# Self-attention in eight blocks, four PSUM banks for the first pass, and inverted sums spread over partitions and multiplied in on POOL

## The reference, cut to what matters

```python
q, k, v = (_heads(q), _heads(k), _heads(v))          # (2, 16, 2048, 32)
attn = jnp.einsum('bhnd,bhmd->bhnm', q, k) * SCALE
attn = jax.nn.softmax(attn, axis=-1)
sa = _merge(jnp.einsum('bhnm,bhmd->bhnd', attn, v)) @ sa_proj_w.T
```

## Time and profile before

| what | us |
|---|---|
| three runs | 3642.99, 3648.21, 3652.91; median 3648.21 |
| the profiled execution | 3647.82 |
| its span, first to last instruction | 3646.0 |
| mean granted TensorE clock | 0.949 of full |

### The profile page before, as it was taken

How to read it: one execution, slowest core, us unless ns; L and a number is a source line. 1 busy time by engine, 2 the same in 40 slices (tenths; PEclk the granted TensorE clock), 3 DMA queues, 4 the chain that set the end, 5 groups by cost and what they waited for, 6 DMA issues and landing times. The chain is left out here.

```text
span 3646.0 us, 52480 instructions
## 1 busy us (share of the span) xinstructions
PE 3342.0 (92%) x16448; PEld 2093.6 (57%) x16448; DVE 2225.3 (61%) x3891; ACT 1551.9 (43%) x2794; POOL 1702.1 (47%) x507
## 2 busy tenths in 40 slices
PE   7998999999999999999999848898967599999999
PEld 5885544444444444444444336656536478888887
DVE  4445888888888878888888234767646532222222
ACT  3230566665666666666666613343432321111111
POOL 0001688887888888888888822343423100000000
PEclk9997999999999999999999968999958799999999
DMA  4447357365465646547444443343325741111110
GB/s 171 182 158 194 62 111 152 85 146 105 88 146 112 132 94 129 121 91 160 99 99 88 99 141 113 117 126 120 102 83 200 254 143 47 47 47 46 46 47 23
DMA packets 179012, 412.02 MB, mean 113 GB/s; under 512 B 20801, under 2 KB 43911, under 8 KB 159343
## 3 DMA queue, kind: packets, MB, share of 16 engines
q1 hardware_dynamic: 156271, 273.87, 24.7%
q0 software_dynamic: 18432, 134.23, 18.3%
q10 hardware_dynamic: 4096, 1.06, 0.1%
HBM read 146.08 MB, written 102.56 MB: 68 GB/s over the span
## 5 line engine op out<-in xcount | busy, mean ns | idle before, releaser
L1653 DVE TENSOR_REDUCE self_part_max<-self_first 128x1 f32<-128x512 f32 x2048 | 1278.1, 676 | 302.9 <-PE self_first L1510 299.6
L1611 ACT ACTIVATE self_expo<-self_second 128x512 f32<-128x512 f32 x2048 | 1068.2, 602 | 693.1 <-PE self_second L1526 654.4
L1459 POOL TENSOR_TENSOR self_pair_sum<-self_expo 128x2048 f32<-128x2048 f32 x192 | 882.9, 4598 | 119.2 <-ACT self_expo L1611 95.3
L1510 PE MATMUL self_first<-self_k,self_q 96*128 96x512 f32 x2048 | 886.0, 440 | 41.4 <-DVE self_part_max L1653 24.5
L1526 PE MATMUL self_second<-self_q,self_k 98*128 98x512 f32 x2048 | 814.7, 401 | 13.9 <-ACT self_expo L1611 13.9
L1510 PEld LDWEIGHTS self_first<-self_k,self_q 96*128 96x128 f32 x2048 | 395.5, 193 | 559.7 <-DVE self_part_max L1653 443.8
L1539 PE MATMUL self_weighted<-self_expo,self_v_sb 128*32 128x512 f32 x4096 | 546.3, 605 | 9.0 <-ACT self_unscaled L1623 6.8
L1526 PEld LDWEIGHTS self_second<-self_q,self_k 98*128 98x128 f32 x2048 | 389.5, 191 | 111.0 <-ACT self_expo L1611 48.7
L2005 DVE CAST mlp_h_high<-mlp_h 128x512 fp32r<-128x512 f32 x128 | 54.8, 428 | 507.9 <-PE mlp_out_sum L61 507.0
L1980 ACT ACTIVATE mlp_h<-mlp_hidden_sum,mlp_b_col 128x512 f32<-128x512 f32 x128 | 88.3, 690 | 603.0 <-PE mlp_hidden_sum L61 603.0
L1459 POOL TENSOR_TENSOR self_half_sum<-self_expo 128x2048 f32<-128x2048 f32 x64 | 293.0, 4583 | 88.2 <-ACT self_expo L1611 88.2
(11 more groups left out here) (165 smaller groups left out, 4180.5 us busy)
## 6 DMA issues: line engine op xcount, KB each, us to landing
self_half_sum<-self_pair_sum POOLq DMA_DIRECT2D x128, 1024.0 KB, 7.2
self_k<-k_t SPq DMA_DIRECT2D x96, 256.0 KB, 9.8
self_q<-q_t SPq DMA_DIRECT2D x93, 256.0 KB, 4.5
cross_q<-cross_r_high SPq DMA_DIRECT2D x256, 64.0 KB, 2.0
qkv_x<-in_x SPq DMA_DIRECT2D x8, 1024.0 KB, 5.4
v<-qkv_v_sb SPq DMA_DIRECT2D x32, 256.0 KB, 2.0
q_t<-qkv_r_high SPq DMA_DIRECT2D x32, 256.0 KB, 2.0
q_t<-qkv_r_low SPq DMA_DIRECT2D x32, 256.0 KB, 2.3
```

Of the source, the lines that this page charges most:

```text
L1459: nc.gpsimd.tensor_tensor(to, expo[:, t % p_slots], expo[:, (t + 1) % p_slots], ALU.add).then_inc(pair_done, 1)
L1510: nc.tensor.matmul(first[:, in_ring[n]], q[0:base, c % q_slots, a, s * P:(s + 1) * P], k[0:base, c // stages_per_group % 2, a, k0:k0 + TOK ...
L1611: nc.scalar.activation(expo[:, t % p_slots, a], second[:, n % ring], ACT.Exp, scale=scale).then_inc(exp_done, 1)
L1653: nc.vector.tensor_reduce(part_max[:, a * SUB + s, k:k + 1], first[:, in_ring[n]], AX_X, ALU.max).then_inc(first_read, 1)
```

## The change

- A stage has eight blocks instead of 16. In each, PE issues eight first-pass and eight second-pass tiles in turn and then weighs two key tiles, those of the block before. DVE and ACT follow the same order.
- The first pass gets a PSUM ring of four banks. The bank `total` is gone: `total` and the turned maxima are now uses of the second pass's ring of three (`s_uses`), so what comes three uses later in that ring waits for their readers. The turn comes after one first-pass tile, at the start of block 6.
- All three sums are added in one go at the end of block 1 of the next stage.
- ACT copies the weighted values into `mean` and, new, `total` into `inverse`. SP gathers one row of it for each head into `sums`, 16 columns on each of 128 partitions (four DMAs). DVE takes one reciprocal of that 128x16 tile in block 3. SP stores it to a DRAM scratch, waits for that, and loads it back into `inverse`, broadcast over the 32 partitions of each head (four DMAs).
- POOL multiplies `mean` by `inverse` (128x512), between its pairs 3 and 4 of the next stage.
- `pair_sum` and `half_sum` become four parts of one buffer, two of which change roles from stage to stage. POOL's wait for its own previous addition (`pair_done`, `n_adds * i`) now stands ahead of pair 0, and its wait for a sum ahead of pair 0 is gone.

The core of the diff:

```diff
-    blocks = n_k
-    per_block = heads
+    blocks = 8
+    per_block = n_seconds // blocks
...
-    turn_after = 2
-    ring = 3
+    turn_after = 1
+    f_ring = 4
+    s_ring = 3
     p_slots = 8
-    pieces = 8
+    share = heads * TOK // P
...
-    sums_at = {15: [(0, 0)], 2: [(-1, 1)], 3: [(-1, 2)]}
-    last_sum, invert_from, max_sent = 3, 5, 13
+    sum_block, take_sum_after = 1, 2 * per_block - 1
+    invert_at, max_sent_after = (3, 1), 55
...
+    def sum_parts(c):
+        return (0, 1, 2, 3) if c % 2 == 0 else (2, 1, 0, 3)
...
+    s_uses = []
+    for j in range(blocks):
+        for at in range(per_block):
+            if first_of[j][at] == (2, turn_after - 1):
+                s_uses.append("turn")
+            s_uses.append(j * per_block + at)
+        if j == sum_block:
+            s_uses.append("total")
+    assert len(s_uses) % s_ring == 0
+    s_slot = {use: p % s_ring for p, use in enumerate(s_uses)}
...
-        pair_sum = m.sbuf("pair_sum", [P, 2, heads, TOK])
-        half_sum = m.sbuf("half_sum", [P, 2, heads, TOK])
+        part_sum = m.sbuf("part_sum", [P, 4, heads, TOK])
...
-        unscaled = m.sbuf("unscaled", [P, TOK])
+        sums = m.sbuf("sums", [P, share])
+        inverse = m.sbuf("inverse", [P, TOK])
         mean = m.sbuf("mean", [P, TOK])
-        first = m.psum("first", [P, ring, TOK])
-        second = m.psum("second", [P, ring, TOK])
+        first = m.psum("first", [P, f_ring, TOK])
+        second = m.psum("second", [P, s_ring, TOK])
         weighted = m.psum("weighted", [P, TOK])
-        total = m.psum("total", [P, TOK])
+        total = second[:, s_slot["total"]]
+        turned_max = second[0:n_max, s_slot["turn"], 0:P]
...
+                def send_sums(i):
+                    ge(sp, total_read, i + 1, alone=True)
+                    for a in range(heads):
+                        rows = slice(a * HEAD_DIM, (a + 1) * HEAD_DIM)
+                        sp.dma_start(sums[rows], inverse[a * HEAD_DIM:a * HEAD_DIM + 1].rearrange("o (j k) -> o j k", k=share)
+                                     ).then_inc(sums_loaded, 16)
+
+                def spread_inverse(i):
+                    ge(sp, inverse_done, i + 1, alone=True)
+                    sp.dma_start(inverse_rows.rearrange("a (j k) -> (a j) k", k=share), sums[:]).then_inc(inverse_stored, 16)
+                    ge(sp, inverse_stored, 16 * (i + 1), alone=True)
+                    for a in range(heads):
+                        sp.dma_start(inverse[a * HEAD_DIM:(a + 1) * HEAD_DIM],
+                                     inverse_rows[a].unsqueeze(0).to_broadcast([HEAD_DIM, TOK])).then_inc(inverse_loaded, 16)
...
+                    if number != 0:
+                        send_sums(i - 1)
                     v_free(0)
                     if number != 0:
+                        spread_inverse(i - 1)
+                    v_free(1)
+                    if number != 0:
                         store_out(r, c - 1)
-                    v_free(1)
                     v_free(2)
...
-                    ge(pool, total_done, n_sums * (i - 1) + 1)
-                    add_pair(i, 0, half_sum[:, 0])
+                def divide(i):
+                    ge(pool, inverse_loaded, 16 * heads * (i + 1))
+                    ge(pool, weighted_read, i + 1)
+                    nc.gpsimd.tensor_tensor(mean[:], inverse[:], mean[:], ALU.mult).then_inc(mean_done, 1)
+
+                def add_pairs(i, c):
+                    h0, h1, p0, p1 = sum_parts(c)
+                    ge(pool, pair_done, n_adds * i)
+                    add_pair(i, 0, part_sum[:, h0])
                     ge(pool, total_done, n_sums * (i - 1) + 2)
-                    add_pair(i, 1, half_sum[:, 1])
-                    ge(pool, pair_done, n_adds * i)
-                    add_pair(i, 2, pair_sum[:, 0])
-                    add_half(i, 2, 0, 0)
+                    add_pair(i, 1, part_sum[:, h1])
+                    add_pair(i, 2, part_sum[:, p0])
+                    add_half(i, 2, 0, h0, p0)
                     ge(pool, total_done, n_sums * i)
-                    add_pair(i, 3, pair_sum[:, 1])
-                    add_half(i, 3, 1, 1)
+                    add_pair(i, 3, part_sum[:, p1])
+                    add_half(i, 3, 1, h1, p1)
+                    if not (isinstance(i, int) and i == 0):
+                        divide(i - 1)
                     ge(pool, half_added[0], 32 * i + 16)
-                    add_pair(i, 4, pair_sum[:, 0])
-                    add_half(i, 4, 0, 0)
+                    add_pair(i, 4, part_sum[:, p0])
+                    add_half(i, 4, 0, h0, p0)
                     ge(pool, half_added[1], 32 * i + 16)
-                    add_pair(i, 5, pair_sum[:, 1])
-                    add_half(i, 5, 1, 1)
+                    add_pair(i, 5, part_sum[:, p1])
+                    add_half(i, 5, 1, h1, p1)
                     ge(pool, half_added[0], 32 * i + 32)
-                    add_pair(i, 6, pair_sum[:, 0])
+                    add_pair(i, 6, part_sum[:, p0])
                     ge(pool, half_added[1], 32 * i + 32)
                     ge(pool, pair_done, n_adds * i + 7)
-                    nc.gpsimd.tensor_tensor(half_sum[:, 1], half_sum[:, 1], pair_sum[:, 0], ALU.add).then_inc(
+                    nc.gpsimd.tensor_tensor(part_sum[:, h1], part_sum[:, h1], part_sum[:, p0], ALU.add).then_inc(
                         pair_done, 1)
...
-                    add_pairs(i)
+                    add_pair(i, 7, part_sum[:, p1])
+
+                add_pairs(0, 0)
+                add_pairs(1, 1)
+                with pool.Fori(1, stages // 2) as r:
+                    add_pairs(2 * r, 0)
+                    add_pairs(2 * r + 1, 1)
+                divide(stages - 1)
...
-                    ge(pe, first_read, slot_free(i, in_ring[n], n))
-                    nc.tensor.matmul(first[:, in_ring[n]], q[0:base, c % q_slots, a, s * P:(s + 1) * P],
+                    ge(pe, first_read, n_reads * i + n - f_ring + (1 if n >= f_ring else 0))
+                    nc.tensor.matmul(first[:, n % f_ring], q[0:base, c % q_slots, a, s * P:(s + 1) * P],
                                      k[0:base, c // stages_per_group % 2, a, k0:k0 + TOK],
...
+                    if before == "turn":
+                        if not (isinstance(i, int) and i - back == stages - 1):
+                            pe.wait_ge(max_split, i + 2 - back)
+                    elif before == "total":
+                        ge(pe, total_read, i - back)
+                    else:
+                        pe.wait_ge(exp_done, n_seconds * i + before + 1 - n_seconds * back)
+
+                def turn_max(r, c):
+                    i = round_stages * r + c
+                    if not (isinstance(i, int) and i == -1):
+                        second_free(i, "turn")
+                    ge(pe, first_read, n_reads * (i + 2))
+                    nc.tensor.transpose(turned_max, row_max[:], identity[:]).then_inc(turned, 1)
...
-                    held = n - ring if n >= ring else (n_seconds - 1 - n) // ring * ring + n - n_seconds
-                    ge(pe, exp_done, n_seconds * i + held + 1)
-                    nc.tensor.matmul(second[:, n % ring],
+                    second_free(i, n)
+                    nc.tensor.matmul(second[:, s_slot[n]],
...
-                def add_up(i, n):
-                    if n == 0:
-                        ge(pe, mean_done, i)
-                        ge(pe, half_added[0], 32 * (i + 1))
-                    elif n == 1:
-                        ge(pe, pair_done, n_adds * i + n_pairs)
+                def add_up(r, c):
+                    i = round_stages * r + c
+                    h0, h1, _, p1 = sum_parts(c)
+                    if isinstance(i, int) and i == stages - 1:
+                        pe.wait_ge(exp_done, n_seconds * stages)
                     else:
-                        ge(pe, pair_done, n_adds * (i + 1))
-                    part = half_sum[:, n] if n < 2 else pair_sum[:, 1]
-                    for a in range(heads):
-                        cols = slice(a * HEAD_DIM, (a + 1) * HEAD_DIM)
-                        mm = nc.tensor.matmul(total[cols], ones[:], part[:, a],
-                                              start=n == 0, stop=n == n_sums - 1)
-                    mm.then_inc(total_done, 1)
+                        second_free(round_stages * r + c + 1, "total")
+                    for n, part in enumerate((h0, h1, p1)):
+                        if n == 0:
+                            ge(pe, half_added[0], 32 * (i + 1))
+                        elif n == 1:
+                            ge(pe, pair_done, n_adds * i + n_pairs)
+                        else:
+                            ge(pe, pair_done, n_adds * (i + 1))
+                        for a in range(heads):
+                            cols = slice(a * HEAD_DIM, (a + 1) * HEAD_DIM)
```

(27 more changed lines are left out.)

92 lines of the change are left out of this document (31 added, 61 removed).

## The result

The changed kernel takes 3611.15 us (median of four runs, 3604.76 to 3612.75) against 3648.86 for the kernel before: a ratio of 0.9887 with a 95% interval of 0.9874 to 0.9901, that is 37.7 us less. The forecast was 3600, its range 3542 to 3646. The profiled execution has a span of 3610.9 us, 35.1 less than the one before.

What follows compares the result with a forecast made beforehand. PE bounded the kernel before; the bound was to move to POOL, 51.7 us a stage. Last sum -67, stalls and clock +4, value loads +6, end +9: -48 from 3648.2, forecast 3600, range 3542 to 3646.

Steps and rivals of the forecast that it cites:

- PE's 49.8 a stage: Self-attention on PE: matmuls, sums, turn and shared total together need 49.8 us a stage, between 49.4 and 50.8.
- change-over of 0.34: PE, between passes and weighing: each change-over costs 0.34 us; eight fewer save 2.7 us a stage.
- POOL's chain of 50.7: POOL's own work in a stage: 49.0 plus 1.15 for the multiply and 0.5 for pair 0's wait, 50.7 us.
- the stretch: POOL's fourth half-add DMA, meeting the next queries' load, lands later: 1.0 us a stage, bounds 0 and 2.7.
- The period is 51.7: Self-attention stage: POOL bounds it, so its chain of 50.7 plus 1.0 for the stretched half-add is the period, 51.7 us.
- +4: Self-attention total: PE's stalls and slow clock at 856 and 1290 us only partly fit in the new slack, +4 us.
- Too short to cost clock: PE at the third sum: it waits 1.9 us a stage for POOL, too short to lower its clock.
- The last sum: End of the self-attention stages: the last third-sum comes at 2031.2 us, -67, before +4 and +6 are added.
- The first: Rival: POOL's half-add is not stretched, the period is its bare chain of 50.7 us, total 3566; chance 0.26.
- the second: Rival: on PE, weighing two tiles in a row costs two change-overs, 52.5 us a stage, about 3628; chance 0.12.
- The third: Rival: POOL's multiply waits for inverses from slow DMA trips; at 7 us a trip, 3814; chance 0.07.
- The fourth: Rival: no difference; half-add stretches by 2.7 or multiply takes 3, period 53.3 or so, 3644; chance 0.11.

Runs made afterwards that it cites:

- e3: The changed kernel with 16 blocks of four heads a stage again instead of eight, all else of the change kept: 3630.1 us.
- e12: The changed kernel with the query and key loads inside the loop cut to 8 columns, the rest stale data: 3577.3 us.
- e2: The changed kernel with SP issuing the queries' load after the sums' transfers instead of at the stage's start: 3597.1 us.
- e7: The changed kernel with queries loaded after the sums' transfers and pair 0 no longer waiting for POOL's own last addition: 3583.9 us.
- e1: The changed kernel with the multiply moved from POOL to DVE, in one piece in block 5: 3650.0 us.
- e5: The changed kernel with the multiply on DVE in four pieces of 128 columns, in four different blocks: 3699.1 us.
- e4: The changed kernel without spreading the inverses: DVE inverts all 512 columns in eight pieces and multiplies in block 6, nine DMAs gone: 3588.6 us.
- e11: The kernel e7 with the next group's keys loaded a head at a time over three stages, behind sums and queries: 3620.5 us.

## Why the prediction was right, and where it was not

- **PE's 49.8 a stage: right.** Measured 49.97. The change-over of 0.34 is 0.33 by e3; the turn's stall 0.32 for 0.35; the row maxima are in time; the shared total and all else take the 0.4 to 0.5 that is left (0.2 in the sum).
- **POOL's chain of 50.7, and 51.7 with the stretch: right as sums, by luck in part.** Measured 50.73 where the loads' bytes are gone (e12), and 51.68 with them. But the sum started from 49.0, one stage of the earlier trace rows, where the mean of the kernel before is 49.57 (bounded by PE, so if anything short), and then added 2.65 where the change added 2.11. Of the three terms the stretch is 0.95 for 1.0 (0.41 of it from the queries by e2; the sum had the queries alone in mind). The multiply was put at its full 1.15, and what leaving it out saves is 0.78 of chain and 0.45 us a stage of time (14.5 / 32), because a wait lay behind it; from its start to the next instruction's it takes 1.24, which is near. Pair 0's wait was put at 0.5, and e7 gives about 0.4.
- **The price by the Trainium skill's GPSIMD Engine Reference, § Engine selection.** POOL needs 1.24 us from the multiply to the next addition against DVE's 0.68 in the earlier trace rows, 1.8 times; the 1.15 that I took from POOL's own additions was a little nearer than the page's twice, 1.36. Its advice to keep such work on VectorE would have been wrong here at the places of e1 and e5 and with both operands in SBUF; in e4, behind the turn, it was not.
- **"The period is 51.7": this step failed**, and it is the larger part of the phase's own miss. The stage is 52.23. POOL's chain was taken as the period, as if POOL never waited for another engine. It does, 0.55 us a stage or 17 us in all: 7.0 of it at the two jumps of the loop (1.59 and 3.63 for PE, twice 0.9 for ACT), for which my "+4" stood, and 10 in other stages. That PE's own stall at a jump would more than double was in no term.
- **"Too short to cost clock": wrong.** PE's waits ahead of the third sum are not 1.9 us in each stage but none in 13 of 31 and 0.3 to 2.9 in the others, and with six of these, the shortest of 1.76 us, the clock fell to 1.2 GHz for 3.4 or 6.8 us. With those at the jumps, and at the half pace that the matmuls above show, 41 us of it are up to 20 us of PE; how much became time is not settled, since POOL was the bound. Two of POOL's three longest waits for exponentials away from the jumps (1.20 us at 718, 2.32 at 1463) come some 27 and 34 us behind the start of a low clock, the third (1.86 at 1039) behind none. No run held the clock and all else fixed.
- **The last sum.** Forecast -67, or -57 with the +4 and +6 of jumps and loads of values; measured -51.5. **The end:** +9 forecast, +6.5 measured: from the copy to the multiply's end 10.6 us for 13.1. The gathering landed after 1.7 us, the store after 1.4 and the broadcast after 2.0, each taken as 2.0; the rest is in shorter hand-overs.
- **The phase as a whole** was forecast at -48 and came at -45.0. The rest of the miss, 8 us of the medians and 9.9 of the profiled executions, is in cross-attention, which the change doesn't touch. With this same code it took between 576.5 and 593.1 us in the 14 profiled executions, and this goes with its low clock: 160 us of it in the shortest (e12), 165 before, 189 in the changed kernel, 196 in the longest (e4), and over all 14 some 0.42 us of time for each us of low clock. Why the clock is low for longer in some executions stays open; one profile of the kernel before can't tell whether the change has a part in it.
- **Rivals.** The first (no stretch) is excluded by e12 and e2, the second (change-overs not saved) by e3. The third (POOL waits for the inverses) did not come in the changed kernel: only two waits, one of them at the end; e11 shows that it was one transfer in the wrong place away. The fourth had the right mechanism, a stretched half-add, at nearly three times the size.
